# Linear attention in an adaLN block: value products replaced by keys times normalised x summed over a batch, and the denominators of units 2 to 4 made in projection steps 13 to 15

## The reference

```
mod = silu(c) @ wmod                        # sa, ca, ga, sb, cb, gb of each batch
h = layernorm(x) * (1 + ca) + sa            # x: 2 batches of 2048 tokens, 256 wide
Q, K, V = h @ Wq.T + bq, h @ Wk.T + bk, h @ Wv.T + bv    # 16 heads of 16
Q, K = elu(Q) + 1, elu(K) + 1
KV = einsum('bshd,bshe->bhde', K, V);  K_sum = K.sum(axis=1)
Z = 1 / (einsum('bshd,bhd->bsh', Q, K_sum) + 1e-6)
x = x + ga * (einsum('bshd,bhde,bsh->bshe', Q, KV, Z) @ Wo.T + bo)
h = layernorm(x) * (1 + cb) + sb
x = x + gb * moe(h)                         # 8 experts of 128, top 2 by cosine + linear score
```

## Time and profile before

| what | us |
|---|---|
| median of 3 runs | 357.65 (357.5 to 357.69) |
| the profiled execution | 357.7 |
| its span, first to last instruction | 355.9 |
| TensorE busy | 340.1 (96%) |
| VectorE busy | 284.8 (80%) |
| GpSimd busy | 261.2 (73%) |
| ScalarE busy | 235.5 (66%) |

### The profile page before, as it was taken

One profiled execution on the slowest core, in us unless ns is written; L12 is line 12 of the kernel. 1 busy time (PEld: TensorE's weight loads), 2 busy tenths in 40 slices (PEclk: granted clock), 3 DMA queues, 4 the chain that ended last, 5 costly groups with the idle time before them and its releaser, 6 DMA issues.

```text
span 355.9 us, 8794 instructions
## 1 busy us (share of the span) xinstructions
PE 340.1 (96%) x2798; PEld 321.1 (90%) x2798; DVE 284.8 (80%) x816; ACT 235.5 (66%) x517; POOL 261.2 (73%) x358
## 2 busy tenths in 40 slices
PE   8889999998999987899999999999999999999895
PEld 8777888887888977799999999999999999999895
DVE  5598676658858889998989998888889897876754
ACT  4686878887877755657658567575585585765541
POOL 4349999977867588788779898898899966755210
PEclk9999999999999999999999999999999999999999
DMA  7956500000000033132142223321322233224311
GB/s 271 333 169 206 159 25 0 1 2 0 2 0 3 4 119 114 36 121 89 64 137 92 72 90 82 129 91 60 127 97 71 90 98 111 91 63 147 100 50 62
DMA packets 23728, 31.82 MB, mean 89 GB/s; under 512 B 2294, under 2 KB 14218, under 8 KB 23692
## 3 DMA queue, kind: packets, MB, share of 16 engines
q1 hardware_dynamic: 23252, 31.34, 28.0%
q10 hardware_dynamic: 440, 0.04, 0.1%
HBM read 27.04 MB, written 4.34 MB: 88 GB/s over the span
## 4 chain that ended last, share of the span: by engine, by line
PE 74%; DVE 13%; issue 4%; ACT 3%; DMA 3%; POOL 2%; SPq 1%; DVEq 0%; POOLq 0%; ACTq 0%
PE bank L820 21%; PE bank L821 20%; PE bank L822 20%; PE bank L828 5%; DMA x_sb<-in_x 3%; PE bank L875 2%; PE bank L1005 2%; PE bank L852 2%; DVE gT_f L1437 1%; PE bank L1047 1%; DVE hid_g L1381 1%; DVE bank L1398 1%; DVE stats L1149 1%; ACT hid_pair L770 1%; ACT e_sb L652 1%
## 5 line engine op out<-in xcount | busy, mean ns | idle before, releaser
L763 ACT ACTIVATE bank<-bank,cols_sb 128x256 f32<-128x256 f32 x128 | 51.6, 440 | 48.2 <-PE bank L822 47.8
L820 PE MATMUL bank<-tr_hi,w_hi 128*128 128x256 f32 x256 | 72.7, 284 | 0.0
L822 PE MATMUL bank<-tr_hi,w_lo 128*128 128x256 f32 x256 | 71.5, 279 | 0.0
L821 PE MATMUL bank<-tr_lo,w_hi 128*128 128x256 f32 x256 | 71.5, 279 | 0.0
L820 PE MATMUL bank<-w_hi,hid_pair 128*128 128x256 f32 x252 | 70.6, 280 | 0.0
L821 PE MATMUL bank<-w_lo,hid_pair 128*128 128x256 f32 x252 | 70.4, 279 | 0.0
L822 PE MATMUL bank<-w_hi,hid_pair 128*128 128x256 f32 x252 | 70.4, 279 | 0.0
L520 POOL TENSOR_TENSOR hid_pair<-hid_g,hid_pair 128x512 fp32r<-128x512 f32 x42 | 55.0, 1309 | 3.1 <-ACT hid_pair L770 1.7
L820 PEld LDWEIGHTS bank<-tr_hi,w_hi 128*128 128x128 f32 x256 | 48.5, 189 | 0.3 <-DVE hid_g L1381 0.2
L821 PEld LDWEIGHTS bank<-tr_lo,w_hi 128*128 128x128 f32 x256 | 48.2, 188 | 0.0
L822 PEld LDWEIGHTS bank<-tr_hi,w_lo 128*128 128x128 f32 x256 | 48.1, 188 | 0.0
(11 more groups left out here) (163 smaller groups left out, 922.7 us busy)
## 6 DMA issues: line engine op xcount, KB each, us to landing
g_bc<-g_dram SPq DMA_DIRECT2D x64, 256.0 KB, 3.5
x_sb<-in_x SPq DMA_DIRECT2D x16, 256.0 KB, 3.1
out<-x_sb SPq DMA_DIRECT2D x15, 256.0 KB, 2.3
early<-in_wmod SPq DMA_DIRECT2D x3, 512.0 KB, 6.7
q_sb<-in_w SPq DMA_DIRECT2D x2, 512.0 KB, 6.3
q_sb<-in_w SPq DMA_DIRECT2D x1, 1024.0 KB, 9.2
mod_row<-mod_dram SPq DMA_DIRECT2D x1, 1024.0 KB, 6.0
q_sb<-in_wqkvT SPq DMA_DIRECT2D x2, 384.0 KB, 5.3
```

The costliest lines, as they stand in the source:

```text
L763: last = ac.activation(half, half, ACT.Gelu, bias=b1_sb[:, e:e + 1])
L820: te.matmul(out_ap, l_hi, r_hi, start=start, stop=False, skip_group_check=shared)
L821: te.matmul(out_ap, l_hi, r_lo, start=False, stop=False, skip_group_check=shared)
L822: return te.matmul(out_ap, l_lo, r_hi, start=False, stop=stop, skip_group_check=shared)
```

## The change

The value product is linear, so the sum over tokens can come first. Each unit now multiplies its keys with its normalised x before modulation (`xk`: four float32 products of 256 columns, all 256 x 256 pairs of features), which TensorE sums in one PSUM bank over the eight units of a batch. After the last unit ScalarE scales that sum with the modulation (`scale_xk`), and TensorE multiplies it with the value weights, four float32 products (`kv_of`), for batch 0 in step 10, for batch 1 in expert step -1. The shift of the modulation and the bias are added with the key sums (`keep_shifts`, `shift_bias`, `mask_kv`). `v`, `kv`, `keep_v` and `add_kv` are gone, and seven fill matmuls of step -1; the value weights are no longer split in two and are loaded after the modulation rows. `nat` has four slots instead of one, statistics are made four units ahead, and GpSimd makes 1/sqrt for two units at once in even steps from step 2. The projection loops are written out. `make_prod` and `denominators` of units 2, 3 and 4 stand in steps 12 to 14 and 13 to 15, with a place of their own for each result; those of unit 5 stand at the end of step 0. The key sums of batch 1 are kept by ScalarE (`keep_ksum_kv`).

```diff
-        kv_b = early[:, 4 * E:4 * E + P].rearrange("p (c n) -> p c n", c=NC)
+        wv_sb = early[:, 2 * E:4 * E].rearrange("p (c n) -> p c n", c=NC)
+        kv_b = early[:, 4 * E:5 * E].rearrange("p (c n) -> p c n", c=NC)
         kv_m = early[:, 5 * E:6 * E].rearrange("p (c n) -> p c n", c=NC)
-        prod = early[:, 6 * E:6 * E + 2 * NH * (D + 1)].rearrange("p (k d) -> p k d", d=D + 1)
+        n_prod = 2 * NH * (D + 1)
+        prod = early[:, 6 * E:6 * E + n_prod].rearrange("p (k d) -> p k d", d=D + 1)
+        xk_sb = early[:, 6 * E + n_prod:6 * E + n_prod + NC * NC * (P + B)].rearrange(
+            "p (c k n) -> p c k n", c=NC, k=NC)
+        Z_AHEAD = 5
+        z_ahead = early[:, 11 * E - Z_AHEAD * 2 * NH:11 * E].rearrange("p (u t h) -> p u t h", u=Z_AHEAD, t=2)
...
+        SLOTS = 4
...
+        nat = sb("nat", [P, SLOTS, 2, E])
+        nat_e = sb("nat_e", [P, 2, E])
...
+        def slot_of(u):
+
+            return u.count() % SLOTS
+
+        def rstd_call(u):
+
+            return u if u < SLOTS else SLOTS + (u - SLOTS) // 2
+
+        def xk_bank(b):
+
+            return bank[6 if b else 4][:, :]
+
+        def kvt(b, c):
+
+            return bank[6][:, E + c * P:E + (c + 1) * P] if b else bank[1][:, c * (P + B):(c + 1) * (P + B)]
+
+        def z_of(u):
+
+            return next((z_ahead[:, j, :, :] for j in range(Z_AHEAD) if u.nth(j)), z[:, :, :])
...
+            sp.dma_start(wv_sb, wqkvT[:, 2 * E:3 * E].rearrange("(c p) n -> p c n", p=P)).then_inc(d_wv, 16)
...
+            def rstd_a(u, n=1):
+
+                wait(pool, a_stats, u.count(1, n))
+
+                wait(pool, a_xn, u.count(1, n - SLOTS))
+                make_rstd(rstd_call(u.count()) + 1, slot_of(u), n, a_eps, a_pow, a_rstd)
...
-                if u.plus(2):
+                if u.nth(0) or u.nth(1):
                     rstd_a(u.plus(2))
+                elif u.plus(2) and not u.h:
+                    rstd_a(u.plus(2), 2)
...
-                if u.nth(UPB + 6):
-                    make_prod(unit(2))
+                if any(u.nth(j) for j in range(UPB + 4, UPB + 7)):
+                    make_prod(u.plus(-2 - UPB))
...
-                    make_prod(u.plus(4))
...
-                if u.nth(-1):
-                    make_prod(u.plus(5))
...
-            def keep_v(u):
-
-                wait(act, a_v, u.count(1, 1))
-                wait(act, a_kv, u.count(1, -1))
-                ac.activation(v_sb[:, u.h, :, :].rearrange("p t e -> p (t e)"), bank[4][:, :], ACT.Copy)\
-                  .then_inc(a_vs, 1)
+            def keep_ksum_kv():
+
+                act.wait_ge(f_ksum, B)
+                act.wait_ge(f_kvt, NC * B)
+                ac.activation(ksum_row[:, 1, :], bank[6][:, 0:E], ACT.Copy)
+                ac.activation(kv_b[:, :, :].rearrange("p c n -> p (c n)"), bank[6][:, E:2 * E], ACT.Copy).then_inc(f_ksrow, 1)
+
+            def scale_xk(b):
+
+                act.wait_ge(a_kv, UPB * (b + 1))
+                wait(act, f_kvm, b)
+                for c in range(NC):
+                    last = ac.activation(xk_sb[:, c, :, 0:P],
+                                         xk_bank(b)[:, c * E:(c + 1) * E].rearrange("p (k n) -> p k n", k=NC), ACT.Identity,
+                                         scale=mod_col[:, 2 + c, b:b + 1])
+                last.then_inc(f_acc, 1)
...
+                if u.nth(UPB + 1):
+                    scale_xk(0)
...
-                keep_v(u)
...
+                if u.nth(0):
+                    keep_ksum_kv()
+                if u.nth(-1):
+                    scale_xk(1)
...
-            def v(u):
-                h = u.h
-
-                wait(pe, a_vs, u.count(1, 0))
+            def xk(u):
+                b, first_of_batch, last_of_batch = u.batch(), u.nth(0) or u.nth(UPB), u.nth(UPB - 1) or u.nth(NU - 1)
+
+                wait(pe, a_fm, u.count(2, 2))
                 for t in range(2):
-                    tok = slice(t * P, (t + 1) * P)
                     for c in range(NC):
-                        last = mm3(bank[4][:, t * E:(t + 1) * E], tr_hi[:, h, c, tok], tr_lo[:, h, c, tok],
-                                   wqkv_hi[:, c, 2 * E:3 * E], wqkv_lo[:, c, 2 * E:3 * E], c == 0, c == NC - 1)
-                last.then_inc(a_v, 1)
-
-            def kv(u):
-                h = u.h
-
-                wait(pe, a_fm, u.count(2, 2))
-                wait(pe, a_vs, u.count(1, 1))
-                wait(pe, a_acc, u.count(1, 1))
-                for c in range(NC):
-                    for t in range(2):
-                        for half in HALVES:
-                            f = slice(c * P + half, c * P + half + 64)
-                            last = te.matmul(bank[6][half:half + 64, c * 64:(c + 1) * 64], v_sb[:, h, t, f],
-                                             k_sb[:, h, t, f], start=(t == 0), stop=(t == 1))
+                        last = te.matmul(xk_bank(b)[:, c * E:(c + 1) * E], nat[:, slot_of(u), t, c * P:(c + 1) * P],
+                                         k_sb[:, u.h, t, :], start=(first_of_batch and t == 0 and c == 0),
+                                         stop=(last_of_batch and t == 1), skip_group_check=True)
                 last.then_inc(a_kv, 1)
+
+            def kv_of(b, c):
+
+                pe.wait_ge(d_wv, 16)
+                pe.wait_ge(f_acc, b + 1)
+                pe.wait_ge(f_shift, 1)
+                for k in range(NC):
+                    last = te.matmul(kvt(b, c), wv_sb[:, k, c * P:(c + 1) * P], xk_sb[:, k, c, 0:P if b else P + B],
+                                     start=(k == 0), stop=(k == NC - 1))
+                last.then_inc(f_kvt, 1)
...
+                if u.nth(UPB + 2):
+                    for c in range(NC):
+                        kv_of(0, c)
...
-                if u.nth(NU - 1):
-                    kv(u.plus(-1))
-                v(u)
-                if u.plus(-1) and not u.nth(NU - 1):
-                    kv(u.plus(-1))
+                if u.plus(-1):
+                    xk(u.plus(-1))
...
-                    kv(unit(NU - 1))
+                    xk(unit(NU - 1))
...
-                    pe.wait_ge(a_acc, NU + 1)
-                    fill(bank[6], 7)
+                    for c in range(NC):
+                        kv_of(1, c)
...
-            pipeline(te, step_a, 2, 4, UPB)
+            for u in range(2, NU):
+                step_a(unit(u))
...
-            def add_kv(u):
-                b = u.batch()
-
-                wait(dve, a_kv, u.count(1, 1))
-                wait(dve, a_acc, u.count(1, 1))
-                acc = kv_acc[:, b, :, :].rearrange("p c n -> p (c n)")
-                TT(acc, acc, bank[6][:, 0:P], ALU.add).then_inc(a_acc, 1)
+            def keep_shifts():
+
+                for c in range(NC):
+                    last = ve.tensor_copy(xk_sb[:, c, :, P:], mod_col[:, c:c + 1, :].to_broadcast([P, NC, B]))
+                last.then_inc(f_shift, 1)
...
-                dve.wait_ge(a_acc, UPB * (b + 1) + 1)
-
+                dve.wait_ge(f_kvt, NC * b + c + 1)
+                made = kv_b[:, c, :] if b else kvt(b, c)[:, 0:P]
+                ve.scalar_tensor_tensor(kv_b[:, c, :], ksum_row[:, b, c * P:(c + 1) * P], bv_all[:, c, b:b + 1],
+                                        made, ALU.mult, ALU.add).then_inc(f_step, 1)
+
+            def shift_bias():
+
+                dve.wait_ge(f_kvt, NC)
+                for c in range(NC):
+                    last = TT(bv_all[:, c, :], kvt(0, c)[:, P:], bv_sb[:, c:c + 1].to_broadcast([P, B]), ALU.add)
+                last.then_inc(f_bv, 1)
+                dve.wait_ge(f_bv, 1)
+
+            def place_kv(b):
+
+                dve.wait_ge(f_step, NC * (b + 1))
                 wait(dve, f_m, b)
-                for half in HALVES:
-                    rows = slice(half, half + 64)
-                    last = ve.scalar_tensor_tensor(kv_b[rows, c, :],
-                                                   ksum_row[rows, b, c * P + half:c * P + half + 64],
-                                                   bv_sb[rows, c:c + 1], kv_acc[rows, b, c, :], ALU.mult, ALU.add)
-                last.then_inc(f_step, 1)
-
-            def place_kv(b):
-
-                dve.wait_ge(f_step, NC * (b + 1))
-                for half in HALVES:
-                    rows = slice(half, half + 64)
-                    mask = head_mask[rows, half:half + 64].rearrange("p (o n) -> p o n", o=1).to_broadcast([64, NC, 64])
-                    last = TT(kv_m[rows, :, half:half + 64], kv_b[rows, :, :], mask, ALU.mult)
-                last.then_inc(f_kvm, 1)
+                mask = head_mask[:, :].rearrange("p (o n) -> p o n", o=1).to_broadcast([P, NC, P])
+                TT(kv_m, kv_b, mask, ALU.mult).then_inc(f_kvm, 1)
...
-                wait(dve, o_qz, u.count(1, 0))
+                if not any(u.nth(j) for j in range(Z_AHEAD + 1)):
+                    wait(dve, o_qz, u.count(1, 0))
```

(27 more changed lines are left out.)

137 lines of the change are left out of this document (67 added, 70 removed).

## The result

The changed kernel takes 354.77 us (median of 4 runs, 354.47 to 355.05), the kernel before 357.67 (4 runs) beside it: a ratio of 0.9913, 95% interval [0.9901, 0.9924], 2.90 us less. Timed once more it was 354.56 (6 runs) against 357.89: 0.9904 [0.9886, 0.9921], 3.33 less. I take 3.1, the mean of the two, for it. Forecast: 354.7. The profiled span is 353.2 us.

A forecast was written before the change was run, and what follows sets the result against it. TensorE's own work was taken to bound both stages, with VectorE's order between them. Gains of 1.6 us through step 11, 1.0 in steps 12 to 15, then the handover and restarts made 3.0: 357.7 to 354.7 us, range 352.4 to 357.3.

The forecast's parts named there:

- The exchange of products: TensorE, each projection unit: loses 1.37 + 0.61 us, gains eight records at 0.215, 1.72; 5.87 becomes 5.61, 0.26 less.
- GpSimd paces the even steps: Steps 3 to 9: GpSimd needs 5.94 us in even steps, two steps 11.43; 5.65 a unit taken, +1.5 over seven units.
- Unit 3: Step 1: VectorE's second statistics and GpSimd's later, longer rstd group make this unit 0.7 us late: -0.7.
- The start: Steps 0 to 2 gain nothing, since TensorE waits for GpSimd; smaller weight load and shorter splits lie beside ScalarE's work: 0.
- Batch 0: Step 10: four added value-weight products cost 0.9 us against the step's own +0.26; step 11: +1.2 and +0.26.
- The gap at the output matrix: Step 11: VectorE's masking shrinks from 2.12 us, so TensorE's 1.02 us gap and its restart go: +1.2.
- Steps 12 to 15: Four units gain 0.26 us each, +1.0; early statistics, q products with key sums and denominators take idle time: 0.
- Handover: Projection to experts: -1.1 and -0.1 for products, +0.5, +1.0 and -0.3 for waits; restarts bring the total from 2.6 to 3.0.
- A: Whole kernel: everything hides, GpSimd never paces, unit 3 and gates in time, 0.92 us wait goes: 352.5 us; chance 0.16.
- B: Even projection steps: GpSimd paces, a pair takes 11.8 us, steps 3 to 9 gain nothing: 356.7 us; chance 0.14.
- C: New products: float32 weight loads do not hide, a record costs 0.275 us, kernel slower at 362.4 us; chance 0.06.
- D: Handover: ScalarE's scaling of batch 1 holds up qz_hi of unit 2 by 1.0 us: 355.7 us; forecast including it 0.56.

The follow-up runs named there:

- experiment 7: The changed kernel with each product of keys with normalised x issued twice (keys twice): 377.47 us, ratio 1.0537 to the kernel before.
- experiment 1: The changed kernel with single deviations, one unit's in every projection step instead of two units' in every other: 352.56 us, ratio 0.9849 to the kernel before.
- experiment 5: The changed kernel with GpSimd's output bias of steps 3, 5 and 7 deferred behind that of steps 4, 6 and 8: 354.25 us.
- experiment 9: The changed kernel with single deviations in every step and the negated mean made on VectorE instead of GpSimd: 354.17 us.
- z ahead only: The kernel before, with only the q.z products and denominators of units 2 to 4 put ahead, in steps 13 to 15: 356.52 us.
- experiment 6: The changed kernel with pairs of deviations before step 10 and single ones from step 10 on: 353.31 us, ratio 0.9865 to the kernel before.
- experiment 2: The changed kernel with no z ahead: q.z products and denominators of units 3 and 4 back in the handover: 355.60 us.
- filled start: The changed kernel with 12 reduced-float32 matmuls of 256 columns into an idle bank in step 0: 354.45 us.
- late pairs: The changed kernel with paired deviations beginning at step 4, not 2, and the second statistics moved from step 1 to step 3: 353.59 us.
- experiment 8: The changed kernel with pairs only in steps 4, 6 and 8, output bias deferred, single deviations from step 10, second expert unit's gate exponent first: 352.80 us.
- experiment 11: The changed kernel with single deviations in every step and the second expert unit's gate exponent ahead of GpSimd's first tr_lo: 352.45 us.

## Why the prediction was right, point by point

- **The exchange of products, -0.26 a unit.** Right in sign, short in size: TensorE's own unit is 5.42, a gain of 0.45. The price of a record was right (0.216 by experiment 7, forecast 0.215). What was wrong is the sum around it. Before, from the first value matmul (65.91) to the next q/k product (67.99) it is 2.08 us, where I summed 1.37 + 0.61 = 1.98: the edge between value and head products was missed. After, eight records take from 60.22 to 61.76, 1.54 rather than 1.72, and the next product's first record is 0.09 longer (0.59, as against 0.50). 2.08 - 1.54 - 0.09 is the 0.45.
- **GpSimd paces the even steps.** Right in kind: 5.42 and 5.72 in turn, shown by experiments 1, 5 and 9. The pair is 11.15 us, not 11.43: TensorE's half is 0.19 less, and GpSimd's chain in an even step, from subtraction to subtraction, 5.82 to 5.84, not 5.94. Seven periods with that of step 9 gained 2.3 us, not 1.5.
- **Unit 3, -0.7.** -1.03 by its period in the first profile, but that holds the low clock. In the second the group starts 0.4 us later than before and takes 0.4 more, as forecast, the product comes at 33.50 (forecast near 33.4), and the bias 0.79 us later than before. Right in mechanism and size.
- **The start, 0 otherwise.** Unit 2 came 0.38 us later than before in the first profile and 0.10 earlier in the second; in two profiles with the start of the kernel before (before and z ahead only) it came at 27.87 and 28.51. No effect of the change can be told from that.
- **Batch 0.** The four added products: -0.85 for 10 to 11, against -0.64, though the step's own gain was 0.45. Their eight records took 0.88 us to the next product, as forecast (0.9), but TensorE waits for VectorE ahead of them, a wait that the prediction did not have:

```profile
75.10 1.24 DVE L1310 COPY early<-mod_col 128x4 f32<-128x4 f32 x2
```

```profile
76.49 1.13 PE L918 MATMUL bank<-early 128*128 128x130 f32 x8 [0.30 <-DVE early L1310]
```

One of the two copies took 0.16 us, the other 1.17, ending 0.03 us after an addition of GpSimd (74.96 to 76.24). The gap at the output matrix: I counted all of 1.02 and a restart as won, with the step's own share 1.46; it gave 0.87, as the mask product (L1353) ran into GpSimd's product: 1.35 us, 0.42 alone, by experiment 6. This is what failed in that step: I read the 2.12 us of the earlier trace rows as the price of two 64x64 instructions and took the new order for cheaper. The eight instructions of that line and shape take 0.18 to 1.30 us, half of them under 0.29, and the two ended at 83.33, 0.08 us after GpSimd's product (81.96 to 83.25). So the 2.12 us was the lock too, as far as rows tell; no run removes it from the kernel before.
- **Steps 12 to 15, +1.0, z work at nothing.** 1.33 for three units at the 0.45 each; the z work is hidden, as experiments 2 and 3 show.
- **Handover, +0.4 in all.** +0.5. qz_lo's wait gave 1.2 for the forecast 1.0, the next wait grew by 0.4 for the forecast 0.3. But the reason given for the last was only half of it: the exponent first takes 0.2 off that wait and nothing off the time. And the sum here counts the restart at the output matrix a second time, since the 1.2 of batch 0 had it already: 0.1 to 0.2 us too much.
- **Rivals.** A and B were each right for a place: the 0.3 us by which even steps are longer is B's, smaller than B had it. C is excluded by experiment 7. D did not appear: none of TensorE's gaps in the handover ends with ScalarE's scaling.
- The misses cancel, by the first profile: +0.8 in units 4 to 10, +0.3 in 13 to 15 and +0.1 in the handover, against -0.4 at the start, -0.3 at unit 3 and -0.2 and -0.6 at batch 0. Single terms were off by up to 0.8 us; that the total was off by 0.1 is partly luck. Of the signs named ahead, the step of 5.6 to 5.7 us did not appear (5.42 and 5.72), and the wait at the output matrix stayed with 0.59 us; attention of unit 3 came 2.94 us earlier, and near 196 us the changed kernel was 2.7 us ahead.

## What to carry to other kernels

Pairing small operations to save an engine's fixed price makes the first of the pair wait for the inputs of the second: here a pair saved GpSimd 1.3 us in two steps (a group of two takes 1.64 us up to the subtraction behind it, one of four 1.96), but it put all of the work into one of the two, which became longer than TensorE's 5.42, and it cost 0.8 us at unit 3 and 0.8 at the mask, so that single ones were 2.2 us faster. When a small operation on VectorE takes several times what its like takes elsewhere in the same trace, look at what GpSimd runs beside it before pricing it by its shape. Price a group that is replaced from the first start of what goes to the start of what follows, not by adding the groups.

## What the runs showed of the hardware that was not expected

**The lock between VectorE and GpSimd** in its numbers: a 128x256 float32 product or subtraction with both inputs in SBUF took 0.42 us, and 1.35 to 1.41 when it began beside a 1.28 us two-input operation of GpSimd (experiments 5 and 6). In both places it ended 0.28 to 0.29 us after GpSimd's operation did. There it had begun about 0.2 us after GpSimd; in the changed kernel's step 11 the same subtraction begins 0.51 us after, is shorter by that, and ends 0.27 us behind it again: a wait, not a slower rate.

```profile
84.91 1.31 POOL L461 TENSOR_TENSOR tr_lo<-tr_f,tr_hi 128x512 fp32r<-128x512 f32 x1 [1.69 <-ACT tr_hi L667]
```

```profile
85.42 1.07 DVE L1325 TENSOR_TENSOR w_lo<-q_sb,w_hi 128x256 fp32r<-128x256 f32 x1
```

Operations of VectorE with one input do the same in these traces: a multiplication of 128x2 by a constant, 0.17 us alone, took up to 1.28 us (experiment 9), and a copy of 128x4 1.17 us in place of 0.16. They ended 0.02 to 0.04 us after GpSimd's operation. The profile shows all this as a long duration and not as a wait.

**The granted clock** fell in the first profile of the changed kernel to 0.50, the 1.2 GHz level, for three microseconds, after TensorE had been busy 0.62 of 2.00 us; in the second profile, with the same idling, it did not, nor with the filled start. Over all 14 profiles: with TensorE busy 0.60 to 0.62 us of the 2.00 the clock fell to 0.50 in seven (also late pairs, bias deferred, keys twice and the experiments 8, 9 and 11) and stayed at 1.00 in four (the second profile, single deviations, no z ahead, single from 10); with 2.00 of 2.00 busy it stayed in all three (before, z ahead only, filled start). Each first row is the idle stretch, the second the one after; first profile, second profile, filled start:

```profile
18.00:20.00 2.00, 0.62 (x5) 0.53 (x5) 1.52 (x5) 1.97 (x5) 1.28 (x1) 1.00 1.00 341
...
21.00:22.00 1.00, 1.00 (x4) 0.80 (x3) 0.97 (x5) 0.00 (x0) 0.00 (x0) 0.50 0.56 134
```

```profile
18.00:20.00 2.00, 0.62 (x3) 0.53 (x4) 1.55 (x5) 1.97 (x5) 1.28 (x1) 1.00 1.03 349
...
21.00:22.00 1.00, 1.00 (x8) 0.84 (x7) 0.94 (x5) 0.69 (x2) 0.29 (x2) 1.00 0.15 46
```

```profile
18.00:20.00 2.00, 2.00 (x25) 1.27 (x23) 1.30 (x4) 1.97 (x5) 1.28 (x1) 1.00 0.97 327
...
21.00:22.00 1.00, 1.00 (x7) 0.77 (x6) 0.96 (x4) 0.00 (x1) 0.00 (x0) 1.00 0.75 217
```

From unit 0 to unit 3 the first took 22.46 us and the second 21.51. Three more profiles have the same start: bias deferred, with the low clock, 22.43; no z ahead and single from 10, without it, 21.59 and 21.52. So it goes with 0.9 us there. Counted from the span's start it is 0.3 to 0.6 us at unit 3 (35.43 and 35.62 against 35.00 to 35.17), since unit 0 came earlier in the two. The idling does not suffice to make the clock fall, since four profiles have it and stay at 1.00; that it is needed is not shown by three profiles without it.
